# A staircase correction for the row maximum, moved from VectorE into a TensorE product, in an ALiBi transformer layer

## The reference, cut to what matters

```python
attn = einsum('bhqd,bhkd->bhqk', q, k) / sqrt(8)
dist = -abs(pos[None, :] - pos[:, None])
attn = softmax(attn + slopes[h] * dist)
x = layernorm(x + einsum('bhqk,bhkd->bhqd', attn, v) @ wo.T + bo)
h = silu(w1 x) * (w2 x)
h = gelu(h1 h); h = gelu(h2 h)
x = layernorm(x + w3 h)
```

## Time and profile before

| | |
|---|---|
| time, three runs | 962.63 us median, 962.04 to 964.39 |
| the profiled execution | span 961.6 us from the first to the last instruction; no other time is shown for it |
| attention | about 0 to 597.7 us, where the first L786 of the feed-forward block starts |
| mean granted TensorE clock | 0.983 of full speed |

### The profile page before, as it was taken

How to read it: one execution, slowest core, us unless ns; L and a number is a source line. 1 busy time by engine, 2 the same in 40 slices (tenths; PEclk the granted TensorE clock), 3 DMA queues, 4 the chain that set the end, 5 groups by cost and what they waited for, 6 DMA issues and landing times. The chain is left out here.

```text
span 961.6 us, 24138 instructions
## 1 busy us (share of the span) xinstructions
PE 911.5 (95%) x6914; PEld 724.1 (75%) x6914; DVE 737.4 (77%) x3039; ACT 654.9 (68%) x1168; POOL 140.6 (15%) x213
## 2 busy tenths in 40 slices
PE   1899999999999999999999996899999999999995
PEld 1677778787787877878778774688888888888883
DVE  5789898888888888888888873667766777776764
ACT  4277676676666766667666764677777777777773
POOL 3002112121211212112121132000010000000101
PEclk9799999999999999999999998899999999999998
DMA  6244443444434344443444420001111111111001
GB/s 176 79 134 114 129 116 109 125 107 129 114 111 126 105 125 117 113 122 106 126 118 116 124 80 20 25 25 45 33 33 33 33 44 42 34 39 37 23 23 44
DMA packets 72307, 80.60 MB, mean 84 GB/s; under 512 B 8208, under 2 KB 68368, under 8 KB 69200
## 3 DMA queue, kind: packets, MB, share of 16 engines
q1 hardware_dynamic: 71392, 77.28, 28.9%
q0 software_dynamic: 880, 2.88, 1.1%
HBM read 45.53 MB, written 33.55 MB: 82 GB/s over the span
## 5 line engine op out<-in xcount | busy, mean ns | idle before, releaser
L614 DVE CUSTOM_DVE_ANT_0 scored<-ps_a,corner_rows 128x256 f32<-128x256 f32 x1024 | 376.1, 418 | 21.7 <-PE ps_a L371 8.6
L524 ACT ACTIVATE probs<-ps_b 128x512 f32<-128x512 f32 x512 | 301.7, 599 | 128.7 <-PE ps_b L362 125.8
L371 PE MATMUL ps_a<-qk_stack 126*128 126x256 f32 x1024 | 255.4, 333 | 17.2 <-DMA qk_stack<-qk_scratch 15.1
L383 PE MATMUL ps_b<-qk_stack 128*128 128x256 f32 x1024 | 209.5, 286 | 2.3 <-ACT probs L524 2.1
L371 PEld LDWEIGHTS ps_a<-qk_stack 126*128 126x128 f32 x1024 | 162.3, 197 | 47.1 <-issue 29.7
L383 PEld LDWEIGHTS ps_b<-qk_stack 128*128 128x128 f32 x1024 | 159.3, 191 | 6.5 <-ACT probs L524 3.8
L848 ACT ACTIVATE gelu_f<-ps_r,sc 128x512 f32<-128x512 f32 x128 | 88.3, 690 | 79.9 <-PE ps_r L789 72.4
L396 PE MATMUL ps_o<-probs,v_aug 128*32 128x256 f32 x2048 | 137.0, 385 | 0.4 <-ACT probs L524 0.4
L362 PE MATMUL ps_b<-corner_sb,idb_sb 128*128 128x158 bf16 x512 | 125.3, 245 | 0.0
L786 PE MATMUL ps_r<-g1h,h_hi 128*128 128x512 f32 x256 | 102.6, 401 | 2.0 <-DVE g1l L913 1.9
L786 PE MATMUL ps_r<-g2h,h_hi 128*128 128x512 f32 x256 | 102.8, 401 | 0.0
(11 more groups left out here) (99 smaller groups left out, 1366.8 us busy)
## 6 DMA issues: line engine op xcount, KB each, us to landing
qk_stack<-qk_scratch SPq DMA_DIRECT2D x64, 384.0 KB
qk_scratch<-x_parts SPq DMA_DIRECT2D x32, 512.0 KB, 3.0
qk_scratch<-x_parts SPq DMA_DIRECT2D x32, 256.0 KB, 3.3
xT_sb<-in_xT SPq DMA_DIRECT2D x32, 128.0 KB, 2.1
x_sb<-in_x SPq DMA_DIRECT2D x32, 128.0 KB, 2.1
x_scratch<-x_sb SPq DMA_DIRECT2D x32, 128.0 KB, 1.7
x_in<-x_scratch SPq DMA_DIRECT2D x32, 128.0 KB, 2.1
x_res<-x_scratch SPq DMA_DIRECT2D x32, 128.0 KB, 2.1
```

The costliest lines, as they stand in the source:

```text
L371: mm = pe.matmul(ps[:, qb * SEQ:(qb + 1) * SEQ], q_stack[par][0:KA, h, qb * P:(qb + 1) * P], k_stack[par][0:KA, h, :], start=(qb == 0), st ...
L383: pe.matmul(ps[:, kb * SEQ:(kb + 1) * SEQ], k_stack[par][:, h, kb * P:(kb + 1) * P], q_stack[par][:, h, :], start=(kb == 0), stop=False, s ...
L524: nc.scalar.activation(probs[:, k % HALF, :], ps_b[k % 2][:], ACT.Exp, scale=slope[k]).then_inc(exp_done, 1)
L614: ins = nc.vector.tensor_tensor_reduce(scored[:, k % 2, qb, :], ps_a[A_BANK[k]][:, qb * SEQ:(qb + 1) * SEQ], corner_rows[:, qb, :], -1.0, ...
```

## The change

`score_max` gets the third product: `add_corner` on the bank of `ps_a`, behind the two matmuls, and `scores_a` is raised by it. VectorE reads the bank once, with one `tensor_reduce` over 2x256 values that takes the plain maximum and negates it. `scored`, `corner_rows`, the memset and the two copies that laid the latter, and VectorE's wait for its own previous maximum are gone.

```diff
             def score_max(b, par, h):
...
                 for qb in range(BLK):
-                    mm = pe.matmul(ps[:, qb * SEQ:(qb + 1) * SEQ], q_stack[par][0:KA, h, qb * P:(qb + 1) * P],
-                              k_stack[par][0:KA, h, :], start=(qb == 0), stop=True,
+                    pe.matmul(ps[:, qb * SEQ:(qb + 1) * SEQ], q_stack[par][0:KA, h, qb * P:(qb + 1) * P],
+                              k_stack[par][0:KA, h, :], start=(qb == 0), stop=False,
                               skip_group_check=True)
-                mm.then_inc(scores_a, 1)
+                add_corner(ps).then_inc(scores_a, 1)
...
-                for qb in range(BLK):
-                    nc.vector.tensor_copy(corner_rows[:, qb, qb * P + STEPS_T:(qb + 1) * P], corner_f[:]).then_inc(corner_laid, 1)
-                dve.wait_ge(corner_laid, 2)
...
-                        wait(dve, max_done, (t + 1) * HEADS + k - 1)
                         wait_apart(dve, scores_a, (t + 1) * HEADS + k + 1, passed["dve"])
-                        for qb in range(BLK):
-                            ins = nc.vector.tensor_tensor_reduce(
-                                scored[:, k % 2, qb, :], ps_a[A_BANK[k]][:, qb * SEQ:(qb + 1) * SEQ], corner_rows[:, qb, :], -1.0, F32_MAX,
-                                ALU.add, ALU.min, negmax[:, k // HALF, k % HALF, qb:qb + 1])
-                        ins.then_inc(max_done, 1)
+                        nc.vector.tensor_reduce(negmax[:, k // HALF, k % HALF, :], ps_a[A_BANK[k]][:].rearrange("p (b k) -> p b k", b=BLK),
+                                                AX_X, ALU.max, negate=True).then_inc(max_done, 1)
...
-            nc.vector.memset(corner_rows[:], 0.0).then_inc(corner_zero, 1)
```

More of the change, by code:

```diff
@@ L64 @@
 CORNER = P - STEPS_T
-F32_MAX = float(np.finfo(np.float32).max)
 QH, QL, KH, KL = range(4)
@@ L203, in attention @@
         xT_sb = [sb(f"xT_sb{i}", [P, SEQ]) for i in range(2)]
-        scored = sb("scored", [P, 2, BLK, SEQ])
         x_sb = [sb(f"x_sb{i}", [P, BLK, D]) for i in range(2)]
         xb_sb = [sb(f"xb_sb{i}", [P, BLK, D]) for i in range(2)]
-        corner_rows = sb("corner_rows", [P, BLK, SEQ])
         negmax = sb("negmax", [P, 2, HALF, BLK])
@@ L234, in attention @@
         spilled = sem("spilled")
-        corner_zero, corner_laid = sem("corner_zero"), sem("corner_laid")
         stacked = [sem(f"stacked{i}") for i in range(2)]
@@ L576, in lay_constants @@
                 dve.wait_ge(const_landed, N_CONST * DMA)
-                dve.wait_ge(corner_zero, 1)
                 nc.vector.tensor_copy(idb_sb[:], id_sb[:]).then_inc(const_set, 1)
                 nc.vector.tensor_copy(corner_sb[:], corner_f[:].unsqueeze(1).broadcast_to([P, BLK, CORNER])).then_inc(const_set, 1)
-                for qb in range(BLK):
-                    nc.vector.tensor_copy(corner_rows[:, qb, qb * P + STEPS_T:(qb + 1) * P], corner_f[:]).then_inc(corner_laid, 1)
-                dve.wait_ge(corner_laid, 2)
             def max_lo(b, hf):
```

## The result

The changed kernel takes 1018.84 us (median of 4 runs, 1018.41 to 1019.66) against 963.41 us for the one before (4 runs, 962.04 to 964.39). The ratio is 1.0591, 95% interval 1.0567 to 1.0615. It is slower by 55.4 us; forecast were 1023 us and a range of 1012 to 1033.

A forecast was written before the change was run, and what follows sets the result against it. The prediction took TensorE to bound the kernel: 59.5 us for 496 added products plus 0.5 for step -1 and 0.5 for the lower clock, 60.5 us over the 961.6 span, gave 1023 us as the median, range 1012 to 1033.

The forecast's parts named there:

- The bound: In the steady attention steps TensorE sets the pace, 17.13 us a step, with no measurable wait for VectorE.
- the gap of 0.4 us: Wait of TensorE's weight loads after the product with v, named "issue" or VectorE; read as not caused by VectorE.
- The price of a slot: Each added staircase product on TensorE costs 0.12 us a head, from the row with the new place's neighbours; 0.60 becomes 0.72.
- the rows at 0.08 and 0.17: Bounds of the price: the staircase before a turn of the outputs and before a product with v; 40 and 84 us.
- The sum for steps 0 to 30: 496 heads at 0.12 us on TensorE, 59.5 us, plus 0.5 us for the lower clock in step 0.
- half-clock term: Start of step 0 at 1.2 GHz: four heads cost 0.11 us more each, 0.5 us.
- The chain before step 0: Step -1: five added products delay the product for q and k and the DMA behind it, 0.5 us.
- VectorE's instruction: VectorE's one new reduction per head takes 0.60 to 0.75 us against 0.69 for the old pair; gains at most 0.09.
- A cheaper slot: Rival: the new load and product partly fall into room on TensorE, 0.08 us each; 41 us more, 1004; chance 0.08.
- VectorE is the bound: Rival: VectorE sets the pace through release of banks, so 0.09 us a head, 45 us, is won; 918; chance 0.03.
- no change: Rival: TensorE had slack that takes all the added work, no measurable change; 963 us; chance 0.02.
- The signal's longer way to VectorE: Rival: staircase before VectorE's signal makes the slot 0.17 us or VectorE hold a bank; 84 + 1 us, 1048; chance 0.05.

The follow-up runs named there:

- TensorE's part: Kernel before, with the staircase product added into ps_a while VectorE keeps its two instructions per head and corner_rows stays zero: 1021.11 us, ratio 1.0631.
- VectorE's part alone: Changed kernel without the staircase product in ps_a, one plain maximum per head: 960.44 us, ratio 0.9995 to the kernel before.
- double run: Changed kernel with a second product of the same shape, its table all zeros, behind the new one: 1051.61 us, ratio 1.0943 to the kernel before.
- adjacent runs: Changed kernel with each new product moved directly ahead of the staircase product of ps_b: 993.65 us, ratio 1.0321 to the kernel before.
- narrow run: Changed kernel with the new staircase product cut from 2x79 to 2x8 columns: 1019.51 us, ratio 1.0607 to the kernel before.
- spread run: Kernel before, nothing added, four of TensorE's side products moved directly behind staircase products of ps_b: 984.62 us, ratio 1.0228.

## Why the prediction was right

**The bound** was read rightly: TensorE sets the pace. The two halves of the change, run alone, show it, with the loss whole in TensorE's part (two steps 38.06) and nothing in VectorE's (34.26). The step that carried this was to see the gap of 0.4 us as one that belongs to the product with v; it is there in every kernel run here that was searched for it, with 0.4 us and one name or the other.

**The price of a slot**, 0.12 taken, is 0.119 from the two-step time. The choice of the row with the right neighbours over the rows at 0.08 and 0.17 mattered, and the double and adjacent runs show why: neighbours are what the price depends on. The bounds were not read like the price, though. 0.08 and 0.17 are distances from the staircase to the next start, and by that reading the chosen row has 0.04 (312.42 to 312.46). The 0.12 came from a subtraction that gives every f32 matmul 0.12, and the prediction did not test that. For the turns the steady 0.11 from one to the next bears the 0.08 out; the 0.17 is a distance alone. In the prediction I wrote that a slot costs about the same whatever its columns; the runs show that only between two f32 pairs.

The section of the Trainium skill that I had set aside (TensorE: Matmul & The Clock Gate, Back-to-back issue gap) gives its formula for a matmul by itself and says that at small sizes it counts too little for a stream with weight loads; the prediction left that out. The 68 ns worked out from it are met in this case's double run (0.067), and the change paid 0.119.

**The sum for steps 0 to 30** was 60.0 with the half-clock term and measured 57.2. At 1.90 us a step the steady pace alone would give 58.9. The rest is small change of the kind I had costed at nothing. In step 30 the kernel before takes 17.14 us and the changed one 18.41, only 1.27 more: VectorE then splits weights beside the maxima, and before, that held TensorE a little: with VectorE's part alone the step takes 16.75. Steps 1 to 3 before are held in the same way, 17.19, 17.29 and 17.29 us, where VectorE's part alone has 17.16, 17.15 and 17.12.

Step 0 took 1.4 us more and not 1.9 + 0.5. The term for the lower clock does show in two heads. The staircases of `ps_b` in the changed kernel at 1.2 GHz:

```profile
36.98 0.36 PE L358 MATMUL ps_b<-corner_sb,idb_sb 128*128 128x158 bf16 x1
38.31 0.36 PE L358 MATMUL ps_b<-corner_sb,idb_sb 128*128 128x158 bf16 x1
39.78 0.36 PE L358 MATMUL ps_b<-corner_sb,idb_sb 128*128 128x158 bf16 x1
```

The second and the third head take 1.33 and 1.47 us, against 1.09 and 1.23 before (39.37, 40.46, 41.69), 0.24 more each, as forecast. But the first head cost nothing more, 1.29 us from the start of the step to its last staircase in both kernels, and the clock rose 5.5 us after the start of the step instead of 5.9.

**The chain before step 0** is the term with the wrong sign: +0.5 forecast, -2.4 found. The chain is as I read it, but its DMAs land at other times in every profile: step 0 starts at 35.09 with VectorE's part alone, at 37.20 with TensorE's, at 37.94 in the narrow run and at 39.30 in the spread run. Part of it is there before any score has been made, since the first product for q starts at 7.78 before and at 7.03 after. Half a microsecond can't be seen in that, and no run here shows that the 2.4 us are the change's. Of the 5.4 us between the 60.5 forecast and the 55.1 found, this term is 2.9 and the steps are 2.8, with 0.3 the other way; both terms made the forecast too high, and the range held the error.

**VectorE's instruction** was bounded at 0.60 to 0.75 a head from start to start and is 0.60, at the lower bound, and its busy share fell to 73%, just under the 75 to 83 I named. In the steady part that bought nothing.

**The rivals.** "A cheaper slot" is refuted for the place the change chose and is real for another order (0.065). "VectorE is the bound" falls with VectorE's part alone, and "no change" with the time. The signal's longer way to VectorE hurt nobody, since even the adjacent order, which delays it further, runs at its computed pace.

## What to carry to other kernels

Before work is moved from one engine to another, find which of the two the third ones wait for: lowering a busy share of 86% next to one of 100% to 77% was worth nothing, and in the steady part each slot added to the full one was paid whole. On a full TensorE, price a product by its neighbours: between two f32 pairs one of 16 columns cost as much as one of 158, and two products with bf16 weights in a row cost less than the same two apart, by 25 us here. Moving side products to better slots pays only while the chain through ScalarE and VectorE that feeds them keeps its distance.

## What the runs showed of the hardware that I had not expected

The price of a product with bf16 weights depends on where it stands: the same 158 columns cost 0.119 us between two f32 pairs and 0.067 or 0.065 beside another such product, and 16 columns cost 0.118 and 0.024. Whether the load behind it or the change between f32 and bf16 weights is what costs stays open. In the changed kernel the loads' own records have 195 and 198 ns for the two f32 ones and 96 and 98 ns for the bf16 ones. The f32 records are longer than the 0.119 us, and in the double run the bf16 load has 0.10 where the added product costs 0.067, so here a load's recorded duration is not the price of its slot.
